# First edge stage: edge constants and gathered target scores added on TensorE in three bf16 parts, block numbers read by eights

## The reference, cut to what matters

```python
feats = jnp.einsum('nd,hdo->hno', x, Ws) + bs[:, None, :]
a_s = jnp.einsum('hno,ho->hn', feats, aw_src)
a_d = jnp.einsum('hno,ho->hn', feats, aw_dst)
score = a_s[:, src] + a_d[:, dst] + aw_e[:, None] * elem[None, :] + ab[:, None]
w = jnp.exp(-jax.nn.relu(score / 20.0))
pooled = jax.vmap(lambda wi, fi: seg(wi[:, None] * fi))(w, feats[:, dst])
row_sum = jax.vmap(lambda wi: seg(wi))(w)
out = pooled / row_sum[:, :, None]
```

## Time and profile before

| what | value |
|---|---|
| time of three runs, median | 2669.74 us (2667.49 to 2671.74) |
| span of the profiled execution | 3152.6 us |
| `stage_edges0` in the profile | from about 643 to 1337 us |
| its 220 steps in the profile | from about 672 to 1337 us |

### The profile page before, as it was taken

How to read it: one execution, slowest core, us unless ns; L and a number is a source line. 1 busy time by engine, 2 the same in 40 slices (tenths; PEclk the granted TensorE clock), 3 DMA queues, 4 the chain that set the end, 5 groups by cost and what they waited for, 6 DMA issues and landing times. The chain is left out here.

```text
span 3152.6 us, 49567 instructions
## 1 busy us (share of the span) xinstructions
PE 1869.4 (59%) x11708; PEld 1332.9 (42%) x11709; DVE 1956.5 (62%) x6206; ACT 1003.7 (32%) x2697; POOL 1696.0 (54%) x1693
## 2 busy tenths in 40 slices
PE   0045555756666666655888628556666666652499
PEld 0023232634444444442777515344444444441377
DVE  8686666467777777774333247566666666677534
ACT  0012221224444444434222215323333333332431
POOL 4777777446666666515665654265655655560200
PEclk9987776867777777856999959755555555555699
DMA  7000000053333333214323321232222222532401
GB/s 203 2 8 10 10 10 12 1 183 88 86 88 88 86 88 88 72 64 147 83 83 79 103 78 29 58 82 78 79 78 79 79 76 78 112 94 55 151 9 33
DMA packets 169043, 231.02 MB, mean 73 GB/s; under 512 B 72072, under 2 KB 127060, under 8 KB 168819
## 3 DMA queue, kind: packets, MB, share of 16 engines
q0 software_dynamic: 69328, 139.28, 16.5%
q1 hardware_dynamic: 99616, 90.61, 10.1%
HBM read 190.39 MB, written 39.38 MB: 73 GB/s over the span
## 5 line engine op out<-in xcount | busy, mean ns | idle before, releaser
L2365 POOL DMA_INDIRECT e_rows<-mid_table,rec x488 | 502.0, 1029 | 384.9 <-PE e_ps_A L2711 140.2
L986 POOL DMA_INDIRECT e_rows<-mid_table,e_rec x440 | 432.9, 984 | 273.5 <-issue 107.1
L256 POOL DMA_INDIRECT mid_sorted<-p_record,p_row x391 | 411.3, 1052 | 201.8 <-issue 116.0
L1172 PE MATMUL e_ps_A<-e_rows,e_hot 128*125 128x260 f32 x880 | 327.7, 508 | 1.5 <-DVE e_rows L1028 1.5
L256 POOL DMA_INDIRECT mid_sorted<-keep_record,keep_row x231 | 227.4, 984 | 183.3 <-PE x_ps_h L1692 79.9
L2711 PE MATMUL e_ps_A<-e_rows,room 128*32 128x65 f32 x3904 | 189.8, 310 | 178.4 <-issue 175.4
L2711 PEld LDWEIGHTS e_ps_A<-e_rows,room 128*32 128x32 f32 x3904 | 134.9, 162 | 230.3 <-issue 227.4
L2631 ACT ACTIVATE room<-room 128x66 f32 x488 | 125.2, 257 | 321.3 <-issue 209.0
L1157 PE MATMUL e_ps_T<-e_identb,e_hot 128*125 128x128 bf16 x440 | 87.0, 291 | 214.2 <-DVE e_hot L1009 108.6
L1172 PEld LDWEIGHTS e_ps_A<-e_rows,e_hot 128*125 128x125 f32 x880 | 197.9, 250 | 29.3 <-DVE e_rows L1028 2.4
L1662 DVE TENSOR_SCALAR x_hT<-x_ps_h,keep_b1T 128x128 f32<-128x128 f32 x256 | 72.1, 344 | 207.0 <-PE x_ps_y L1701 188.9
(11 more groups left out here) (615 smaller groups left out, 4507.5 us busy)
## 6 DMA issues: line engine op xcount, KB each, us to landing
mid_expert_in<-p_zrow SPq DMA_DIRECT2D x1, 8192.0 KB
w<-in_L_ffn_w SPq DMA_DIRECT2D x16, 512.0 KB
x_w<-in_L_ffn_w SPq DMA_DIRECT2D x16, 512.0 KB
x_y<-in_L_ffn_b SPq DMA_DIRECT2D x64, 128.0 KB
x_xs<-mid_expert_in SPq DMA_DIRECT2D x64, 128.0 KB
mid_expert_out<-x_y SPq DMA_DIRECT2D x64, 128.0 KB
f_w_all<-in_L_ffn_W SPq DMA_DIRECT2D x16, 512.0 KB
e_rows<-mid_table,rec POOLq DMA_INDIRECT x488
```

Source lines behind the costliest of these rows:

```text
L256: pool.indirect_dma_start(out=to, out_offset=bass.IndirectOffsetOnAxis(ap=row[:, t:t + 1].bitcast(U32), axis=0), in_=record[:, t, :], in_o ...
L986: pool.indirect_dma_start(out=rows[:, s % RING * 2 + j, :], out_offset=None, in_=k["table"], in_offset=bass.IndirectOffsetOnAxis(ap=rec[:, ...
L1172: last = nc.tensor.matmul(ps_A[0:NP, q % 4, 0:ROW], hot[:, q * 2 + j, :], rows[:, q * 2 + j, :], start=j == 0, stop=j == 1)
L2365: pool.indirect_dma_start(out=rows[:, j, q, :], out_offset=None, in_=k["table1"], in_offset=bass.IndirectOffsetOnAxis(ap=rec[:, i * TG + q ...
```

## The change

`const` and the target scores are split into three bf16 parts each, as `source` was before. The parts of the target score lie behind its row in the table: a row grows from 260 to 262 f32 numbers (`WROW`), with 12 bf16 parts in the last six. They are written by one DMA of their own after the loop of the projection. TensorE adds both to the source scores in PSUM with two more matmuls against the identity, the second after a wait for the gathered rows; VectorE's `scores` is then the reduction alone. ScalarE reads the block numbers of eight steps at once into eight registers, at `q == 0`. `const` now lies in the memory of `state`, which is cleared later.

```diff
+SPLIT0 = 3
+PARTED = SPLIT0 * H // 2
+WROW = D + PARTED
...
-        feat = m.sb("feat", [NP, ROW])
+        feat = m.sb("feat", [NP, D])
+        a_dst = m.sb("a_dst", [NP, TN, H])
+        dst_parts = m.sb("dst_parts", [NP, TN, SPLIT0, H], BF16)
...
+            sp.wait_ge(s_parts, 1)
+            sp.dma_start(k["table"].rearrange("(p t) d -> p t d", p=NP)[:, :, D:],
+                         dst_parts[:].rearrange("p t c h -> p t (c h)").bitcast(F32)).then_inc(s_tab, 16)
...
+            for n in range(SPLIT0):
+                o.done(nc.vector.tensor_copy(dst_parts[:, :, n, :], a_dst[:]))
+                o.settle()
+                if n + 1 < SPLIT0:
+                    o.done(nc.vector.tensor_tensor(a_dst[:], a_dst[:], dst_parts[:, :, n, :], ALU.subtract))
+                    o.settle()
+            dve.sem_inc(s_parts, 1)
             sorted_rows(o, running[:, 0], whole[:], rest[:], slot[:], G1_N)
...
             def scores(s, q, i):
 
-                sc = score[:, q % 2]
                 wait_alone(dve, s_E, s + 1)
-                o.done(nc.vector.tensor_reduce(sc, ps_E[(q - 3) % 4].rearrange("p a (c h) -> p a h c", c=PARTS), AX, ALU.add))
-                o.settle()
-                o.done(nc.vector.tensor_tensor(sc, sc, const[:, bass.ds(s * 2, 2), :], ALU.add))
-                dve.wait_ge(s_rows[q], i * 32 + 32)
-                o.settle()
-                nc.vector.tensor_tensor(sc, sc, rows[:, q * 2:q * 2 + 2, D:], ALU.add).then_inc(s_sc, 1)
+                nc.vector.tensor_reduce(score[:, q % 2], ps_E[(q - 3) % 4].rearrange("p a (c h) -> p a h c", c=PARTS), AX, ALU.add
+                                        ).then_inc(s_sc, 1)
...
+            o.settle()
+            for n in range(PARTS):
+                o.done(v.tensor_copy(const3[:, :, n, :], const))
+                o.settle()
+                if n + 1 < PARTS:
+                    o.done(v.tensor_tensor(const, const, const3[:, :, n, :], ALU.subtract))
+                    o.settle()
+            v.memset(state[:, RING - 1, :], 0.0).then_inc(s_const, 1)
+            dve.wait_ge(s_const, 3)
...
-                block_of = act.value_load(k["bin0"][0:1, bass.ds(s, 1)], min_val=0, max_val=G0_BINS - 1)
...
+            def blocks(s, n):
+                return nc.values_load_multi_w_load_instructions(
+                    k["bin0"][0:1, bass.ds(s, n)], engines=[mybir.EngineType.Activation], min_val=0, max_val=G0_BINS - 1,
+                    skip_runtime_bounds_check_because="each is a count of blocks begun, less one")[1]
...
+                if i is not None and q == 0 and not (isinstance(i, int) and i == 0):
+                    held[:] = blocks(s - 4, RING)
+                elif isinstance(i, int) and s == 4:
+                    held[:] = [None] * 4 + list(blocks(0, 4))
                 if not (isinstance(i, int) and s < 4):
-                    keep(s - 4, (q - 4) % RING)
+                    keep(s - 4, (q - 4) % RING, held[q])
...
+                at = ps_E[(q - 3) % 4]
                 for j in range(2):
-                    last = nc.tensor.matmul(ps_E[(q - 3) % 4][:, j, :], hotT[:, q % 2, j, :],
-                                            source3[:, bass.ds(s, 1), :, :].rearrange("p a c h -> p (a c h)"),
-                                            start=True, stop=True)
-                last.then_inc(s_E, 1)
+                    nc.tensor.matmul(at[:, j, :], hotT[:, q % 2, j, :], source3[:, bass.ds(s, 1), :, :].rearrange("p a c h -> p (a c h)"),
+                                     start=True, stop=False, skip_group_check=True)
+                nc.tensor.matmul(at, identb[:], const3[:, bass.ds(s * 2, 2), :, :].rearrange("p a c h -> p a (c h)"),
+                                 start=False, stop=False, skip_group_check=True)
+                pe.wait_ge(s_rows[q], i * 32 + 32)
+                nc.tensor.matmul(at, identb[:], rows[:, q * 2:q * 2 + 2, D:].bitcast(BF16),
+                                 start=False, stop=True, skip_group_check=True).then_inc(s_E, 1)
```

More of the change, by code:

```diff
@@ L444, in stage_project0 @@
         s_tab = m.sem("table_written")
+        s_parts = m.sem("score_parts")
         s_kvd = m.sem("kv_done")
@@ L894, in stage_edges0 @@
         RING = 8
-        PARTS = 3
+        PARTS = SPLIT0
         AHEAD = 3
@@ L899, in stage_edges0 @@
         abb = m.sb("abb", [P, H])
-        const = m.sb("const", [P, G0_TILES, H])
+        const3 = m.sb("const3", [P, G0_TILES, PARTS, H], BF16)
         index = rec[:, 0:G0_TILES, 0].bitcast(I32)
-        rows = m.sb("rows", [P, 2 * RING, ROW])
+        rows = m.sb("rows", [P, 2 * RING, WROW])
         hot = m.sb("hot", [P, 2 * RING, NP])
@@ L905, in stage_edges0 @@
         score = m.sb("score", [P, 2, 2, H])
-        state = m.sb("state", [NP, RING, ROW])
+        whole_state = m.sb("state", [P, RING, ROW])
+        state = whole_state[0:NP]
+        const = whole_state[:].rearrange("p r d -> p (r d)")[:, 0:G0_TILES * H].rearrange("p (t h) -> p t h", h=H)
         acc = k["acc0"]
@@ L1050, in _ @@
             v.tensor_copy(index, rec[:, 0:G0_TILES, 0]).then_inc(s_idx, 1)
-            o.done(v.memset(state[:, RING - 1, :], 0.0))
             o.done(v.memset(same[:, 0:1], 0.0))
@@ L1081, in _ @@
             dve.sem_inc(s_srck, 1)
-            peeled = o.n
             def step(s, q, i):
                 first, over = i is not None and isinstance(i, int), i is None
-                if first:
-                    o.n = peeled + 2 * s
-                elif not over and q == 0:
-                    o.enter(i - 1, 2 * RING)
                 if not (first and s < 1 or over and s > G0_N):
@@ L1105, in step @@
                     accumulate(s - 3, (q - 3) % RING)
-                if not first and not over and q == RING - 1:
-                    o.leave(G0_N // RING - 1)
             turns(dve, step, range(3))
@@ L1129, in step @@
                     act.wait_ge(s_a, s + 1)
-                    nc.scalar.activation(rows[:, q * 2:q * 2 + 2, D:], score[:, q % 2], ACT.Exp, scale=-1.0).then_inc(s_w, 1)
+                    nc.scalar.activation(rows[:, q * 2:q * 2 + 2, D:ROW], score[:, q % 2], ACT.Exp, scale=-1.0).then_inc(s_w, 1)
                     if before_end(s + 2):
@@ L1171, in add_up @@
                 for j in range(2):
-                    last = nc.tensor.matmul(ps_A[0:NP, q % 4, 0:ROW], hot[:, q * 2 + j, :], rows[:, q * 2 + j, :],
+                    last = nc.tensor.matmul(ps_A[0:NP, q % 4, 0:ROW], hot[:, q * 2 + j, :], rows[:, q * 2 + j, 0:ROW],
                                             start=j == 0, stop=j == 1)
@@ L1211, in _ @@
             pe.wait_ge(s_srck, 1)
-            source_scores(0, 0)
+            source_scores(0, 0, 0)
             transpose(2, 2)
@@ L3241, in build @@
             "attended1": dram("attended1", [B1 * G1_BINS, D]),
-            "table": dram("table", [NN, ROW]),
+            "table": dram("table", [NN, WROW]),
         }
```

24 lines of the change are left out of this document (12 added, 12 removed).

## The result

The changed kernel takes 2691.15 us (median of 4 runs, 2687.65 to 2695.77); the kernel before takes 2668.61 us beside it (4 runs, 2667.13 to 2671.74). The ratio is 1.0083, 95% interval 1.0071 to 1.0096: 22.5 us slower. The forecast was 2640 us, and its range ended at 2680.

What follows compares the result with a forecast made beforehand. VectorE's order was taken to set the 3.05 us step, the gathers 0.5 us under it. Terms -114 + 16 + 51 + 8 = -39 us on a 3152.6 us span, scaled to the timed 2669.7, gave 2637, stated as 2640 us; range 2590 to 2680.

Steps and rivals of the forecast that it cites:

- What bounds the kernel now: Changed stage's steps: VectorE's order sets the 3.05 us step, the gathers stand 0.5 us under it.
- something else: Part of the 3.05 us mean step beyond VectorE's 2.39 us chain: 0.66 us, seen in VectorE's and ScalarE's idle time.
- VectorE's two additions: Removing L1019 and L1022 from VectorE's path saves 0.52 us a step over 220 steps: -114 us.
- Two more matmuls: TensorE's added matmuls take 0.15 us a step, paid in about half the steps: +16 us.
- The wait for the gathered rows: Moves from VectorE to TensorE one step earlier; no wait while the step stays over 2.54 us: 0 us.
- the cover: Steps longer than the gathers' 2.54 us, with rows landing several steps ahead, hide TensorE's wait for rows.
- Block numbers by eights: ScalarE's eight loads together every eighth step delay VectorE's weighing by 1.9 us, 27 times: +51 us.
- loads overlap: Rival: ScalarE's eight reads cost no more than one, so 51 us come back; 2594 us, 18% chance.
- The preparation: Three casts and two subtractions over 1760 elements on VectorE before the first one-hots, hidden by nothing: +8 us.
- The gathers are the bound already: Rival: gathers already set the timed step at 2.54 us, so only the preparation shows; 2678 us, 22% chance.
- TensorE became no bound: Refers to the rival that slow-clock TensorE sets the step at 2.74 us; 2662 us, 18% chance.

Runs made afterwards that it cites:

- e6: Kernel before, each step's second tile read by a plain DMA of fixed rows instead of a gather; slow chip: 2994.76 us, 0.9602 of before.
- e1: Kernel before, unchanged, profiled again on another chip: 2672.49 us, span 2670.8 us.
- e7: Changed kernel, each step's second tile read by a plain DMA of fixed rows instead of a gather; slow chip: 2850.60 us, 0.9144 of before.
- e4: Changed kernel with block numbers read one per step again: 2695.35 us, 1.0087 of before.
- e3: Kernel before with three casts and two subtractions over 1760 elements added to its preparation, results unused: 2680.43 us, 1.0038 of before.
- g1: Changed kernel with the weighing's second input taken from PSUM, exponentials written twice by ScalarE: 2678.72 us, 1.0038 of before.
- g2: Kernel before with the clearing of the sums in the preparation moved from VectorE to ScalarE: 2664.01 us, 0.9985 of before.
- g4: Changed kernel with the weighing's second input from PSUM and the sums cleared on ScalarE: 2672.04 us, 1.0011 of before.
- e8: Changed kernel with a VectorE clearing of 400 unused numbers ahead of each weighing; slow chip: 3150.53 us, 1.0105 of before.
- e9: Changed kernel with the weighing cut into two instructions; slow chip: 3154.57 us, 1.0127 of before.
- e11: Changed kernel with the score's reduction made three times; another slow chip: 3174.93 us, 1.0098 of before.
- e13: Changed kernel with the weighing in two halves, on another slow chip: 3182.55 us, 1.0116 of before.

## Why the prediction was wrong

**What bounds the kernel now** is the part that failed, in its last sentence: "VectorE's order sets the step, the gathers stand 0.5 us under it". Both numbers were right as such (e6 has the one, 2.44 us; the gathers' 1.27 us the other), but the 0.66 us of "something else" on top belonged to the kind of chip that was profiled. In the timed runs a step was the two gathers' 2.55 us (2 x 1.2748). The warning stood in the text: a timed run shorter by 483 us "and nobody says where". I scaled the whole by 1.18, as if every stage and every term shrank alike. By the stages of e1 they don't: the first edge stage went from 694.1 to 582.3 us, the second from 901.5 to 707.6, the gate stayed at 64.

**VectorE's two additions, -114 us.** They left VectorE's path as worked out: the one-hot follows the reduction by 0.18 us (903.99 to 904.17). They were worth 0, because VectorE didn't set the step; it now waits 99 us in 157 steps for TensorE, 0.63 us each. e7 against e6 shows the gain where the gathers are out of the way.

**Two more matmuls, +16 us.** In order of time, the next instruction starts 0.05 us behind the first of them:

```profile
903.68 0.18 PE L1190 MATMUL e_ps_A<-e_const,e_identb 128*128 x1
903.71 0.18 PE L1193 MATMUL e_ps_A<-e_rows,e_identb 128*128 128x24 bf16 x1
903.73 0.45 PE L1180 MATMUL e_ps_T<-e_identb,e_hot 128*125 128x128 bf16 x2
```

That is 0.05 us for both instead of 0.15, off the path besides. The estimate by the Trainium skill's page "TensorE: Matmul & The Clock Gate", 0.21 us a step, is further off.

**The wait for the gathered rows, 0 us,** with "if the cover goes, the step becomes the gathers' 2.54 us". In the timed runs the cover was not there. And what the moved wait costs was not a wait: it ties the weighing to the gathers' starts, and 105 of 423 gathers are held instead of 19 in e1, 15.4 us more in all. No term stood for that, and it is two thirds of the loss. I never asked what a VectorE instruction does to a GpSimd instruction that starts beside it, though the earlier trace rows has the gathers at a mean of 982 ns beside the 960 of the earlier trace rows.

**Block numbers by eights, +51 us.** Measured: nothing (e4). The source line 1132 in the changed kernel, instructions, ns min/median/max:

```profile
L1132 ACTq TENSOR_LOAD <-keep_bin x28: 527/546/559, 623.7 to 1168.2; - x28
L1132 ACTq FUSED_REGOPS  x26: 46/46/46, 629.9 to 1147.6; - x26
```

Eight numbers are one load of 0.55 us, not eight of 0.35; and it starts at 917.54 beside the 0.70 us activation of L1154 that started at 917.50. That is the "loads overlap" rival's assumption, and it was right in its fact.

**The preparation, +8 us.** Right: 6.75 us in the profile, e3 shows it alone. The casts took 1.08 and the subtractions 1.99 us, 7.2 us in all:

```profile
593.42 1.08 DVE L1074 CAST e_const<-e_state 128x1760 bf16<-128x1760 f32 x1
594.53 1.99 DVE L1077 TENSOR_TENSOR e_state<-e_state,e_const 128x1760 f32<-128x1760 f32 x1
```

Four gathers beside the constants, the casts and the subtractions took 1.51 to 2.92 us (590.59 to 598.05), which cost nothing, since the ring was full before the first adding up.

**The rivals.** "The gathers are the bound already" named the mechanism and its point (a timed step under 2.6 us, and it was 2.55) and gave 2678 us; its 8 us are there as 6.75. It had 22% and should have led. It missed 2691 by 13 us, about what the held gathers cost (14.2 us of pace). TensorE became no bound.

What is shown: the gathers are the bound on the chips of 2669 us (in e1 GpSimd is busy or in the 0.30 us ahead of a gather for 404 of 410 us, and the pace falls to 1.2583 us when g1 makes them shorter), while e7 against e6 shows on another chip that VectorE's saving is there when half of the gathers are gone; the preparation counts in full in the stage (e3, g2, g4); the longer gathers come from the weighing's second SBUF input (g1). That the moved wait brings the weighing there is read from the two traces alone: e8, e9, e11 and e13, which moved, cut or delayed the weighing, ran only on slow chips and did not bear it out. Open: what stops TensorE and VectorE on the other kind of chip, and why `stage_edges1` has 5.6 us more of held gathers in g1.

## What to carry to other kernels

When a profile's span is not the timed median, the two may not have the same bound: work out the step from the timed runs before one engine is named, and don't scale the sum. An engine that is freed only moves its idle time if another one stands a few per cent below it; here 0.52 us a step became waiting, and the setup that paid for it was all that showed. When GpSimd issues gathers back to back, ask of each VectorE instruction with two inputs in SBUF whether a gather starts inside it, and take one input from PSUM where there is room. Don't fill the time ahead of it with a `memset`: that held gathers as well (e8).

## What the runs showed of the hardware that was not expected

- A gather that starts inside a VectorE `tensor_tensor` with both inputs in SBUF (0.68 us) ends 1.50 to 1.52 us behind that instruction's start, up to 0.45 us late; one that is under way when the `tensor_tensor` starts is not longer (0.95 us), except with VectorE full (e7: 1.80 us for 49 that start 0.01 us ahead of it). The `tensor_tensor` is never held. With one input from PSUM no gather is held, at the same 0.68 us of VectorE.
- A `memset` of 128x400 f32 in SBUF, which has no input, holds gathers too: 62 of 64 that start inside it (e8).
- Chips differ by 17 to 18% on this kernel, 2668 us against 3118 and 3146, stage by stage unevenly. The granted clock of the span was lower on the slower ones (0.73 to 0.76 against 0.80 to 0.81), as cause or as effect; the gate, in which GpSimd does nothing, took the same time on both. On one of the slower ones the same change made no difference (0.9997).
- Eight values read into eight registers are one recorded load of 0.55 us.
- With instructions added to one stage's loop a later, unchanged stage was longer by 5.6 us on one kind of chip (longer gathers), and by 23 to 35 us on the other (idle time).
